# A decoder layer on one Trainium2 core: the expert layer computes for each token its two experts only, in 23 blocks of 128 rows

## The chip, the cores and the metric

The kernel runs on one core of one Trainium2 chip. A core has TensorE (PE, matrix products), VectorE (DVE), ScalarE (ACT), GpSimd (POOL) and SyncE (SP), which issues transfers; POOL issues transfers too. The metric is the device time of one run in microseconds (us), as the median of several runs, lower is better.

## The reference, cut to what matters

One decoder layer over x of 4 batches x 256 tokens x 128 features, all in fp32: self attention with 16 heads and fixed-point rounding, cross attention over a context of 1601 rows per batch with 16 heads of 8 features, and then a gated layer with 8 experts. This change is about the third part, with one edit in the second.

```python
x = x + attention(layernorm(x)); x = x + cross_attention(layernorm(x), ctx)
h = layernorm(x)                                  # 1024 tokens of 128 features
gout = h @ Wgate + bgate                          # 8 numbers per token
topv, topi = top_k(gout, 2); topw = softmax(topv)
combine = sum(one_hot(topi, 8) * topw[..., None]) # two non-zero weights of eight
z = (h @ W1 + b1) * (h @ W2 + b2)                 # per expert, 128 -> 256
g = z @ Wg + bg                                   # per expert, 256 -> 256
o = g * sigmoid(g) * (z @ Wl + bl)
y = o @ W3 + b3                                   # per expert, 256 -> 128
x = x + sum_e combine_e * y_e
```

## The kernel before

The whole layer is one program with a hand-written order on each engine, and semaphores between them. Tokens lie in tiles of 128 on the partitions (8 tiles).

**Self attention** fills the first 260 us or so. At its end ACT looks whether the mask is all zero (`mask_probe`), POOL makes one number of it (`partition_all_reduce`, L573) and then clamps the masks (`mask_clamp`, L579), and PE reads that number into a register (L950) and branches into one of two copies of the cross attention, with and without the mask. The two mask tiles of a batch come by `mask_load` (L566).

**Cross attention** (`cross_attention`) has 16 groups (4 batches x 4 groups of 4 heads). A first pass finds each query row's largest score: PE computes 13 pairs of score chunks per group (`chunks`, L826; 12 full pairs of 2 x 512 keys and a short one of 8 x 65, the thirteenth), and DVE reduces each pair to its maxima (`chunk_maxima`, L1377 and L1379). The pairs go through two PSUM buffers in turn, `pair[0]` and `pair[1]`; a table (`slot_table`) numbers the uses ("slots") on both engines. When a group's 13 pairs are done, DVE takes the row maxima (L1383), POOL splits them into three bf16 parts (`split_maxima`, L588 to L592), four pairs later (`SETTLED`) PE transposes these in a slot of their own (`maxima_T`, L847), DVE copies the result out (`maxima_move`, L1390), and SP writes it under the group's queries (`shift_load`, L488). The second pass, some 22 pairs behind (`LEAD`), recomputes the scores transposed with the maxima subtracted (`tile_scores`, L870), ACT exponentiates them (`tile_exp`, L1167), and PE multiplies with the values (`tile_values`, L895). It is cut into 277 events; three pairs of the first pass are put into every four events. At event `X2_AT` DVE normalises the first three batches for the expert layer. The last batch is finished after the events (`finish_tiles`, L908, L914, L919, with L1404 to L1416 on DVE).

**The expert layer before** is dense: every expert is computed for every token. For each of 8 experts and each of 2 halves of 512 tokens (m = 0..15) PE does `up` (L963, features on the partitions, 512 tokens as columns), ACT adds a bias, DVE multiplies (L1434); `gate_linear` (L972), ACT's SiLU (L1200), DVE (L1440); `down` (L981), and DVE adds the weighted result (`add_expert`, L1448). PE's `up` of the next m is put between the halves of this m's `gate_linear`. The weights of an expert (896 KB) come from HBM by SP into one of two places while the previous ones are used. Gates, top 2 and the combining weights (L996, L1462 to L1487) are computed once at the start of this part, and PE's first products hide them. b3 is added by one extra product with the combining weights (L1012, L1503). Every fp32 product shows as two records in the trace, every transpose as one.

## Time and profile before

| | |
|---|---|
| median of 3 runs | 829.4 us (829.07 to 832.95) |
| profiled execution | 831.66 us, its span 829.6 us |
| PE busy in the span | 684.3 us (82%) |
| DVE busy | 533.8 us (64%) |
| ACT busy | 451.6 us (54%) |
| POOL busy | 133.1 us (16%) |
| mean granted clock of PE | 0.944 of full speed |
| moved by DMA | 52.83 MB |

The span is the time from the first to the last instruction of one profiled execution. Busy shares are means over stages with different limits, so each stage has to be looked at by itself. L12 is line 12 of the kernel before.

### The profile page before, as it was taken

How to read it: one execution, taken by the hardware profiler on the slowest of the kernel's cores; microseconds unless marked ns; L12 is line 12 of the kernel's file. 1: busy time of each engine (PE TensorE's matmuls, PEld its weight loads, DVE VectorE, ACT ScalarE, POOL GpSimd, SP SyncE). 2: the span in 40 equal slices, each digit the busy share in tenths (PEclk: the TensorE clock that was granted, in tenths of full speed). 3: DMA queues.
4: the chain of work that ended last, by engine and by line, in shares of the span. 5: the costliest groups of instructions: out<-in, count | busy, mean ns of one | idle time of the engine just before them, and what ended most of it. 6: DMA issues, size and time to landing. Idle time of an engine off the chain costs nothing.

```text
span 829.6 us, 13514 instructions
## 1 busy us (share of the span) xinstructions
PE 684.3 (82%) x5026; PEld 335.3 (40%) x5026; DVE 533.8 (64%) x868; ACT 451.6 (54%) x766; POOL 133.1 (16%) x167
## 2 busy tenths in 40 slices
PE   2763488888878379998899899899869999999996
PEld 2442255555547033333333333333234554544544
DVE  4377789888896958888888788887033333333332
ACT  2552368888892038876787677778832221122121
POOL 5236601000003522401511140000000000000000
PEclk8796789999999569999999999999889999999999
DMA  6323365445121020106111700001100111101100
GB/s 190 131 68 134 102 224 164 118 118 131 41 76 46 0 79 2 42 2 149 71 42 32 189 2 2 1 2 47 45 2 0 45 45 45 28 16 44 44 1 25
DMA packets 30647, 52.83 MB, mean 64 GB/s; under 512 B 3838, under 2 KB 23882, under 8 KB 30148
## 3 DMA queue, kind: packets, MB, share of 16 engines
q0 software_dynamic: 3424, 26.23, 11.8%
q1 hardware_dynamic: 27172, 25.89, 10.1%
q8 instruction: 35, 0.57, 0.3%
q14 instruction: 16, 0.13, 0.0%
HBM read 39.71 MB, written 12.00 MB: 62 GB/s over the span
## 4 chain that ended last, share of the span: by engine, by line
PE 58%; DVE 25%; ACT 8%; issue 6%; DMA 2%; SPq 0%; DVEq 0%; ACTq 0%
PE pair L972 14%; PE pair L895 11%; DVE smax L1377 10%; PE pair L870 6%; DVE region_p L1286 5%; PE pair L826 5%; PE pair L963 5%; PE pair L981 4%; PE pair L730 3%; DVE region_p L1256 3%; PE pair L694 2%; ACT region_p L1167 2%; ACT region_p L1086 2%; PE pair L716 2%; DVE region_p L1289 1%
## 5 line engine op out<-in xcount | busy, mean ns | idle before, releaser
L1377 DVE TENSOR_REDUCE smax<-pair 128x2 f32<-128x1024 f32 x192 | 225.4, 1220 | 50.1 <-PE pair L826 50.0
L1167 ACT ACTIVATE region_p<-pair 128x1024 f32<-128x1024 f32 (+3 forms) x277 | 217.7, 812 | 63.6 <-PE pair L870 57.9
L972 PE MATMUL pair<-region_p,region_g 128*128 128x512 f32 x256 | 118.7, 607 | 2.5 <-DVE region_p L1440 2.3
L1200 ACT ACTIVATE region_p<-pair,bias_T 128x512 f32<-128x512 f32 x32 | 22.0, 687 | 122.2 <-PE pair L972 122.2
L1440 DVE SCALAR_TENSOR_TENSOR region_p<-pair,bias_T,region_p 128x512 f32<-128x512 f32 x32 | 24.0, 751 | 97.6 <-ACT region_p L1200 97.6
L730 PE MATMUL pair<-ident,region_p 128*128 128x128 f32 x256 | 38.5, 298 | 46.0 <-DVE region_p L1289 46.0
L1256 DVE SCALAR_TENSOR_TENSOR region_p<-region_p 128x1024 int16<-128x1024 int16 (+1 forms) x56 | 67.1, 1220 | 14.0 <-ACT region_p L1072 11.6
L972 PEld LDWEIGHTS pair<-region_p,region_g 128*128 128x128 f32 x256 | 46.6, 192 | 62.5 <-issue 55.1
L895 PE MATMUL pair<-region_p 128*32 128x256 f32 (+1 forms) x832 | 67.6, 398 | 0.5 <-ACT region_p L1174 0.4
L895 PE MATMUL pair<-region_p,v_aug 128*32 128x256 f32 (+1 forms) x832 | 66.5, 391 | 0.4 <-ACT region_p L1174 0.4
L826 PE MATMUL pair<-region_k,qstack 56*128 56x512 bf16 (+1 forms) x256 | 44.2, 365 | 23.9 <-DVE smax L1377 22.5
L963 PE MATMUL pair<-xnT,region_g 128*128 128x512 f32 x128 | 60.9, 598 | 0.0
L1286 DVE TENSOR_SCALAR region_p<-region_p,rnorm 128x256 f32<-128x256 f32 x128 | 59.3, 527 | 1.1
L870 PE MATMUL pair<-qstack,region_k 59*128 59x256 bf16 (+1 forms) x416 | 54.3, 272 | 4.1 <-ACT region_p L1167 2.9
L730 PEld LDWEIGHTS pair<-ident,region_p 128*128 128x128 f32 x256 | 30.3, 151 | 60.3 <-DVE region_p L1289 59.2
L1086 ACT ACTIVATE region_p<-region_p 128x256 f32<-128x256 int16 x128 | 51.3, 409 | 0.0
L1434 DVE SCALAR_TENSOR_TENSOR region_p<-pair,bias_T,region_p 128x512 f32<-128x512 f32 x32 | 24.0, 751 | 32.9 <-ACT region_p L1192 32.9
L1192 ACT ACTIVATE region_p<-pair,bias_T 128x512 f32<-128x512 f32 x32 | 22.0, 687 | 38.3 <-PE pair L963 38.3
L741 PE MATMUL pair<-region_p 128*64 128x256 f32 x256 | 34.7, 392 | 9.8 <-ACT region_p L1094 8.2
L1094 ACT ACTIVATE region_p<-pair 128x1024 f32<-128x1024 f32 x32 | 32.5, 1016 | 15.3 <-PE pair L730 15.3
L716 PE MATMUL pair<-region_p 64*128 64x256 f32 x256 | 38.2, 417 | 2.4 <-ACT region_p L1078 1.8
L1078 ACT ACTIVATE region_p<-pair 128x1024 int16<-128x1024 f32 x32 | 32.7, 1022 | 12.5 <-PE pair L716 12.1
(172 smaller groups left out, 903.3 us busy)
## 6 DMA issues: line engine op xcount, KB each, us to landing
kimg<-region_k SPq DMA_DIRECT2D x56, 200.1 KB
region_k<-kimg POOLq DMA_DIRECT2D x8, 1400.9 KB, 12.4
mask_sb<-in_mask_Bx1xSxS_ff POOLq DMA_DIRECT2D x12, 800.5 KB, 5.2
region_p<-in_mask_Bx1xSxS_ff POOLq DMA_DIRECT2D x4, 800.5 KB, 13.2
region_g<-in_L_ffn_W SPq DMA_DIRECT2D x24, 128.0 KB, 2.2
region_g<-in_L_ffn_Wg SPq DMA_DIRECT2D x8, 256.0 KB, 2.9
region_g<-in_L_ffn_Wl SPq DMA_DIRECT2D x8, 256.0 KB, 3.1
wnat<-in_L_attn_w_qkv SPq DMA_DIRECT2D x8, 192.0 KB, 7.2
```

What stands on the lines that cost most here:

```text
L716: last = pe.matmul(pair[0][:, h * 512 + t * 256:h * 512 + (t + 1) * 256], qf[rows, b * S + t * 128:b * S + (t + 1) * 128], kf[rows, b * S: ...
L730: last = pe.transpose(pair[1][:, c:c + 128], attn[:, b % 2, a:a + 128], ident[:, :])
L826: last = pe.matmul(out_, qstack[b][64 * a:64 * a + KROWS, 2 * g + j, q * 128:(q + 1) * 128], kstack[64 * a:64 * a + KROWS, b % 2, 2 * g + ...
L870: last = pe.matmul(st_bank[n % 3][0:rows, j * 256:(j + 1) * 256], kstack[64 * a:64 * a + SROWS, b % 2, 2 * g + j, keys], qstack[b][64 * a: ...
L895: last = pe.matmul(pair[3][32 * h:32 * h + 32, 512 + s % 2 * S:512 + (s % 2 + 1) * S], v_heads[b % 2][0:rows, t, c:c + 32], pT[0:rows, n / ...
L963: last = pe.matmul(pair[f][:, n * 512:(n + 1) * 512], w[:, u, f * 128:(f + 1) * 128], xnT[:, c * 512:(c + 1) * 512], start=True, stop=True)
L972: last = pe.matmul(pair[2][:, n * 512:(n + 1) * 512], w[:, u, f, half * 128:(half + 1) * 128], zed[:, c, f, :], start=(f == 0), stop=(f == 1))
L1086: last = act.activation(expd[:, b % 2, k * 256:(k + 1) * 256], dotf[:, b % 2, k * 256:(k + 1) * 256], ACT.Exp, scale=1.0 / FXP, accum_out= ...
L1167: act.activation(pT[0:rows, first // 3 % 2, k:k + size], home[0:rows, 0:size], ACT.Exp).then_inc(expt_made, 1)
L1256: return dve.scalar_tensor_tensor(out_, floor16, 0.0, floor16, ALU.is_lt, ALU.add)
L1286: last = dve.tensor_scalar(attn_h[:, b % 2, k * 256:(k + 1) * 256], expd[:, b % 2, k * 256:(k + 1) * 256], rnorm[:, k:k + 1], -0.5, ALU.mu ...
L1377: dve.tensor_reduce(units[:, :, c // 3, c % 3], both, AX.X, ALU.max).then_inc(slot_done, 1)
```

## The change

**Routing.** DVE makes gates, top 2, weights and, new, each token's two row numbers in a buffer in HBM (`route`, in two parts: the first 6 tiles during the last cross attention events, the last 2 after them). The rank of a token inside its expert comes from PE (`ranks`: products of 0/1 matrices in bf16). Expert e owns the rows from 1024 e on. POOL writes each normalised token, with its destination's number behind it as a 129th word, to its two rows by indirect DMA (`dispatch`: 16 transfers of 128 rows; 12 in the first part, 4 in the second). `totals` and some 12 small DVE steps make a table of 23 blocks (the most that 2048 rows in 8 experts padded to 128 can need): first row and expert.

**The blocks.** For each block SP reads its first row into a register and loads 128 rows; PE transposes them, and multiplies them as the stationary side with W1 and W2 side by side (512 columns), with Wg and Wl side by side (2 x 512 columns), and with W3 (2 x 128 columns); the expert's number, read from the table into a register of PE and of DVE, addresses weights and biases. Tokens are now on the partitions, so the biases are added from copies broadcast over all partitions, and z and o are transposed back by PE and moved by ACT. POOL writes each block's 128 result rows to their tokens' places by an indirect DMA. At the end SP reads both results of every token (1 MB), DVE adds them with their weights, and SP writes the output in two halves.

**Weights.** All eight experts are resident: Wg and Wl (4 MB) are loaded by POOL at the start of the cross attention, W1, W2, W3 (3 MB) and the broadcast biases (4 MB) when its fourth batch is under way (`experts_load`, put behind `split_maxima(14)`). To make room, buffers are laid over each other otherwise.

**Filling the buffer.** Before, on POOL: two transfers of zeros over the HBM buffer (4.65 MB together) behind the mask probes of u = 5 and 6, and one transfer of 9088 single words (the numbers of rows that hold no token) behind `mask_load(0)`.

**Short pair fifth.** The short pair of a group (8 x 65 keys) is now the fifth of its 13, and the transposed maxima of the group before are written into the free columns of its buffer: one slot instead of two. The separate maxima slots go; the transpose comes with pair 17 + 13 s instead of behind pair 16 + 13 s.

The core of the diff:

```diff
-SETTLED = 4
+TAIL_AT = 4
+UNITS = tuple(range(TAIL_AT)) + (KT - 1,) + tuple(range(TAIL_AT, KT - 1))
+X2_AT = event_of(2 * (KT * (GROUPS - 2) + KT - 2)) - 2
+XNT_AT, GATE_AT, WEIGHTS_AT, RANK_AT = X2_AT + 5, X2_AT + 9, X2_AT + 12, X2_AT + 14
@@ SP
-            with sp.Fori(1, NE // 2) as r:
-                for u in range(2):
-                    sp.wait_ge(y_mm, 4 * r - 2 + 2 * u)
-                    expert_load(sp, 2 * r + u, u)
+            sp.wait_ge(table_made, 1)
+            sp.wait_ge(dispatched, 16 * 2 * NT)
+            for j in range(NBLK):
+                row = sp.value_load(table[0:1, 0, j:j + 1], min_val=0, max_val=ROWS - 128)
+                if j >= RING_X:
+                    i = j - RING_X
+                    sp.wait_ge(ydisp_written[i % RING_Y], 16 * (i // RING_Y + 1))
+                sp.dma_start(xblk[:, j % RING_X, :], xdisp[bass.ds(row, 128), :]).then_inc(xblk_loaded[j % RING_X], 16)
...
+                    sp.dma_start(ytok[:, k, tiles, :], y_tiles[k, :, tiles, :]).then_inc(ytok_loaded[half], 16)
@@ POOL
+            pool.dma_start(xdisp[:, D:ROW].rearrange("(n p) c -> p (n c)", p=128), pad_index.bitcast(F32),
+                           allow_slow_non_contiguous=True).then_inc(pads_written, 16)
...
+            pool.wait_ge(qstack_made, B)
+            pool.wait_ge(pads_written, 48)
+            for n, w in enumerate((Wg, Wl)):
+                pool.dma_start(wgl.rearrange("p (r f) -> p r f", r=2 * NE)[:, :, n * FF:(n + 1) * FF],
+                               w.rearrange("e (k p) f -> p (e k) f", p=128)).then_inc(experts_loaded, 16)
...
+                for t in range(*FFN_TILES[part]):
+                    for k in range(2):
+                        pool.indirect_dma_start(xdisp, bass.IndirectOffsetOnAxis(ap=slots[:, k, t:t + 1].bitcast(U32), axis=0),
+                                                xrow[:, t, k, :], None, ...).then_inc(dispatched, 16)
+            for j in range(NBLK):
+                pool.wait_ge(yblk_made, j + 1)
+                pool.indirect_dma_start(ydisp, bass.IndirectOffsetOnAxis(ap=xblk[:, j % RING_X, D:ROW].bitcast(U32), axis=0),
+                                        yblk[:, j % RING_Y, :], None, ...).then_inc(ydisp_written[j % RING_Y], 16)
@@ PE
+                    if maxima_with(p) is not None:
+                        last = maxima_T(s - 1, home)
...
+            for j in range(NBLK + 2):
+                if j < NBLK:
+                    up(j)                    # value_load; 1 product of 512 columns
+                if j >= 2:
+                    ogl_transposes(j - 2)    # 2 transposes
+                if j + 1 < NBLK:
+                    block_T(j + 1)           # 1 transpose
+                if 1 <= j <= NBLK:
+                    gate_linear(j - 1)       # 2 products of 512 columns
+                if j < NBLK:
+                    zed_transposes(j)        # 2 transposes
+                if j >= 2:
+                    down(j - 2)              # 2 products of 128 columns
@@ ACT, per iteration
+                ogl_move(j - 2); block_move(j + 1); zed_move(j); gate_silu(j - 1); y_move(j - 2)
@@ DVE
+            def zed_of(j):
+                expert[j] = dve.value_load(table[0:1, 1, j:j + 1], min_val=0, max_val=NE - 1)
+                dve.wait_ge(up_mm, j + 1)
+                chain.step(dve.tensor_tensor(upb, up_bank[j % 2], bias_bc[:, bass.ds(expert[j] * (4 * FF), 2 * FF)], ALU.add))
+                dve.tensor_tensor(zed[:, j % 2, :], upb[:, 0:FF], upb[:, FF:2 * FF], ALU.mult).then_inc(z_made, 1)
+            def gl_bias(j):
+                dve.tensor_tensor(glb[:, j % 2, :], gl_bank[j % 2], bias_bc[...512 columns], ALU.add).then_inc(glb_made, 1)
+            def ogl_of(j):
+                dve.tensor_tensor(ogl[:, j % 2, :], silu[:, j % 2, :], glb[:, j % 2, FF:2 * FF], ALU.mult).then_inc(ogl_made, 1)
+            for j in range(NBLK + 1):
+                zed_of(j); gl_bias(j - 1); ogl_of(j - 1)
```

(In the ACT and DVE loops the bounds on j are left out here.)

## Rows read from the trace of the kernel before

**Rows 1.** Windows: length, busy us of PE, PEld, DVE, ACT, POOL (instructions), clock, DMA.

```profile
304.00:604.00 300.00, 268.49 (x3035) 95.24 (x3033) 226.02 (x253) 225.58 (x297) 52.70 (x99) 0.98 0.17 43
606.50:826.00 219.50, 211.38 (x696) 106.91 (x696) 74.73 (x177) 49.55 (x71) 0.00 (x0) 0.98 0.09 26
```

**Rows 2.** Chain that ended last, stage of the experts: start us, us, what.

```profile
604.11 2.45 issue
...
619.58 5.23 PE pair L972 x8
...
651.41 3.67 PE pair L972 x8
655.08 1.72 PE pair L963 x4
656.80 1.96 PE pair L981 x16
```

**Rows 3.** Groups by line, 304 to 604 us: busy us, mean ns, idle before.

```profile
L847 PE MATMUL pair<-identb,nparts 128*24 128x128 bf16 x15 | 3.3, 217 | 8.7 <-DVE smax L1377 8.7
```

**Rows 4.** Chain in the cross attention.

```profile
395.80 3.72 DMA qstack<-nmT
```

**Rows 5.** Groups by line and form, 606 to 830 us.

```profile
L972 PE MATMUL pair<-region_p,region_g 128*128 128x512 f32 x256 | 118.7, 607 | 2.5 <-DVE region_p L1440 2.3
...
L981 PE MATMUL pair<-region_g,region_p 128*128 128x128 f32 x256 | 32.8, 281 | 0.6 <-DVE region_p L1440 0.4
...
L1448 DVE SCALAR_TENSOR_TENSOR x_in<-pair,comb,x_in 128x128 f32<-128x128 f32 x64 | 18.0, 344 | 7.7 <-PE pair L981 7.7
...
L665 PE MATMUL pair<-ident,xn 128*128 128x128 f32 x2 | 0.4, 302 | 1.3 <-DVE xn L1251 1.3
L1405 DVE TENSOR_TENSOR region_p<-pair,rsum_x 128x256 f32<-128x256 f32 x1 | 0.4, 426 | 0.0
...
L1053 ACT ACTIVATE xnT<-pair 128x256 f32<-128x256 f32 x1 | 0.4, 385 | 0.8 <-PE pair L665 0.8
```

**Rows 6.** Chain: one hand-over from PE by ACT and DVE back.

```profile
680.62 0.70 ACT region_p L1200
...
681.45 0.76 DVE region_p L1440
682.21 0.12 issue
```

**Rows 7.** Groups on DVE, ACT, POOL, whole span.

```profile
L1337 DVE SCALAR_TENSOR_TENSOR region_p<-pair,bproj_fx 128x512 int16<-128x512 f32 x1 | 0.7, 692 | 3.8 <-PE pair L780 3.8
...
L552 POOL DMA_DIRECT2D mask_sb<-in_mask_Bx1xSxS_ff x8 | 4.5, 566 | 122.9 <-ACT mask_sb L1099 95.5 <-DMA kimg<-region_k 27.1 <-POOL v_aug L535 0.3
...
L416 POOL DMA_DIRECT2D v_next<-in_ctx x2 | 2.3, 1138 | 0.6 <-POOL region_p L535 0.3 <-POOL v_aug L535 0.3
...
L573 POOL PARTITION_ALL_REDUCE mask_flag<-mask_any  x1 | 0.4, 378 | 8.2 <-issue 8.2
```

**Rows 8.** DMA issues: KB each, median us to landing.

```profile
region_g<-in_L_ffn_W SPq DMA_DIRECT2D x24, 128.0 KB, 2.2
...
v_next<-in_ctx POOLq DMA_DIRECT2D x2, 768.0 KB, 5.8
...
out<-x_in SPq DMA_DIRECT2D x1, 512.0 KB, 3.2
```

**Rows 9.** Timeline around the flag and PE's register read.

```profile
262.51 8.69 POOL L579 TENSOR_SCALAR mask_sb<-mask_sb 128x1601 f32<-128x1601 f32 x2 [7.18 <-issue]
262.53 3.79 PE L780 MATMUL pair<-wpT,region_g 128*128 128x128 f32 x32
...
266.25 0.60 PE L826 MATMUL pair<-region_k,qstack 56*128 56x512 bf16 x4
```

**Rows 10.** Windows for the clock (columns of rows 1).

```profile
220.00:240.00 20.00, 14.53 (x113) 9.94 (x111) 18.95 (x42) 18.19 (x46) 0.53 (x1) 1.00 0.13 41
...
304.00:310.00 6.00, 6.00 (x20) 1.96 (x18) 1.84 (x2) 0.15 (x1) 0.00 (x0) 0.55 0.00 0
```

More of the change, by code:

```diff
@@ L1033, in _, with block_T @@
-            repeat(pe, NE // 2, two_experts)
+                last = pe.transpose(pair[0][0:NE, t * 128:(t + 1) * 128], comb[:, :, t], ident[:, :])
+            last.then_inc(comb_T, 1)
+            pe.wait_ge(combT_made, 1)
+            for t in range(NT):
+                last = pe.matmul(pair[3][:, t * 128:(t + 1) * 128], combT[:, t, :], b3_sb[:, :], start=True, stop=True)
+            last.then_inc(b3_mm, 1)
+            expert = [None] * NBLK
+            def block_T(j):
+                pe.wait_ge(xblk_loaded[j % RING_X], 16 * (j // RING_X + 1))
+                wait(pe, xblkT_made, j)
+                pe.transpose(xT_bank, xblk[:, j % RING_X, 0:D], ident[:, :]).then_inc(xblk_T, 1)
@@ new lines, in down @@
+            def down(j):
+                pe.wait_ge(oglT_made, j + 1)
+                wait(pe, yblk_made, j)
+                for f in range(2):
+                    last = pe.matmul(y_bank, oglT[:, j % 2, f * 128:(f + 1) * 128],
+                                     w3_sb[:, bass.ds(expert[j] * (2 * D) + f * D, D)],
+                                     start=(f == 0), stop=(f == 1))
+                last.then_inc(y_mm, 1)
+            pe.wait_ge(table_made, 1)
+            pe.wait_ge(experts_loaded, 16 * 9)
```

623 lines of the change are left out of this document (386 added, 237 removed).

## The prediction

> **What bounds the kernel now.** I read the windows first. From 606.5 to 826 us PE is busy 211.4 of 219.5 us [rows 1]: the expert stage is bound by PE, and DVE (74.7) and ACT (49.6) wait for it. The chain of what ended last shows its content: a half of `gate_linear` (8 records) takes 3.4 to 3.7 us, a half of `up` 1.72, `down` 1.96 [rows 2]. Two of each of the first two and one `down` are 12.4 us, and 16 such steps 198 us. The rest is the first 12 us (tail of the last batch, gates) and bubbles. A record of 512 fp32 columns takes 0.43 us (3.44 / 8 or 1.72 / 4), so an fp32 product of 512 columns 0.86; one of 128 columns 2 x 0.12 = 0.245 (1.96 / 8). The cross attention from 304 to 604 us has PE at 268.5 of 300 us, DVE and ACT at 226 each [rows 1]: PE mostly, with stalls of which 8.7 us stand in front of the 15 maxima transposes, each in a slot that waits for DVE [rows 3]. Self attention is hardly touched.
>
> **PE's work in the new expert stage.** Dense means 16 x 512 x 8/8 = 8192 token-expert rows; now there are 23 x 128 = 2944, 36%. Per block: `up` 0.86, `gate_linear` 2 x 0.86 = 1.72, `down` 2 x 0.245 = 0.49, and new five transposes of one record, about 0.11 each, 0.55. Sum 3.62 us, x 23 = 83 us instead of 198.
>
> **But PE will not set the pace; the cycle through the engines will.** A block goes PE, ACT, PE, DVE, PE, ACT, PE, DVE, ACT, DVE, PE, ACT, PE, ACT, POOL. PE's order lets three blocks overlap, but `ogl_transposes(j-1)` stands ahead of `gate_linear(j)` and needs what follows from `gate_linear(j-1)`. That closed cycle is: bias add of 512 columns on DVE 0.69 [rows 7], SiLU of 256 columns on ACT 0.39 (as the copy of 256 columns [rows 5]), product of 256 on DVE 0.43 [rows 5], two transposes 0.24 and `block_T` 0.12 on PE, `gate_linear` until its result is there 3 x 0.43 + 0.61 = 1.90 [rows 5]. Sum 3.77, plus four hand-overs. The chain shows 0.12 to 0.14 between ACT, DVE and PE where registers address operands [rows 6]; I take 0.15 for each, 0.6. Period 4.4 us. DVE's own sum is 2 x 0.69 + 2 x 0.43 = 2.24, ACT's about 1.9, so neither binds. The clock: a stretch with PE busy 14.5 of 20 us had the full 2.4 GHz granted, and a stretch that began cold ran at 0.55 over 6 us [rows 10]. With 3.6 of 4.4 busy I take full clock, after a cold start that costs 3 us.
>
> **One block alone** takes: transpose 0.30, ACT 0.27 (128 columns, an estimate from 0.39 for 256), `up` 0.43 + 0.61, DVE 0.69 + 0.43, two transposes 0.44, ACT 0.39, `gate_linear` 1.90, DVE 0.69, ACT 0.39, DVE 0.43, 0.44, ACT 0.39, `down` 0.65, ACT 0.27 and 13 hand-overs of some 0.08: 9.7 us. Loop: 9.7 + 22 x 4.4 + 3 = 109.5 us.
>
> **From the end of the cross attention to the first block**, in the clock of before. The 2.45 us after 604.11 (PE leaving the branch) stay [rows 2]. The tail of the last batch loses the `up` halves put into it: xn is there at about 614.1 instead of 616.7. Transpose, ACT and the gates of two tiles: 615.5. The routing was hidden behind PE's first products (the 5.23 us piece at 619.58 [rows 2]); now it stands on the path, for 2 tiles instead of 8: some 15 dependent DVE steps of about 0.2 us with ranks between them, 4.1 us: row numbers at 619.6. Four indirect DMAs follow. No row shows one. Nearest below: a plain transfer of 128 rows occupies POOL 0.57 us, one of 1536 pieces 1.14 [rows 7]; above: POOL's only special instruction, 0.38 with 8.2 idle before it, 8.6 [rows 7]. It is nearer to a transfer with 128 pieces whose addresses are read one by one; I take P = 1.2. 12 of the 16 start at about 599.6 (`ranks(0)` stands at event 269 of 277, the events to 604 are 1.06 us each, and DVE has some 9 short steps after it), and are hidden up to P = 20 / 12 = 1.7. So 619.6 + 4.8, landing 2.2 (128 KB [rows 8]): 626.6. Meanwhile DVE makes the table (12 steps of 0.25) and the b3 term (1.2, from 692 ns for 512 columns): hidden, unless P is under 0.6. SP's register read and issue 0.7, landing 2.2: first block at 629.5.
>
> **After the loop:** loop end 739.0; last scatter 1.2 + 2.2; SP issues 4 transfers, 1 MB at the rate of 768 KB in 5.8 us is 7.7 us [rows 8]: 750.1; 8 weighted adds of 0.28 (18.0 / 64 [rows 5]) for the second half 2.3; output 0.4 + 3.2 [rows 8]: 756.
>
> **Cross attention.** Removed: 16 slots. Of the 8.7 us in front of them I count all, since the short pair's slot waits anyway; the DVE copy moves into a slot. Added on PE in the last events: gates 1.5 (12 records of 0.12) and ranks 0.6. The maxima come with pair 17 instead of behind 16: 1.3 us later plus 0.7 for the short pair's reduction. Before, a shift transfer beside a heavy load took 3.72 us and was waited for [rows 4], one of two such waits; now four groups (beside Wg/Wl at 301, keys twice, the 7 MB at 559) may wait 1 us or so more each, half of it caught up. Net -8.7 + 2.1 + 2 = -5 us, between -12 and +4. The 7 MB are issued behind `split_maxima(14)`, 7 POOL transfers of 0.9 to 1.4 us; even at 132 GB/s (768 KB in 5.8 us [rows 8]) they land within 53 us, by 612, ahead of need at 629. What is queued behind them on POOL is `split_maxima(15)`, due a group later (300 / 16, 18 us).
>
> **Filling the buffer.** The two transfers of zeros lie where DMA has room, 18 us each at that rate, and nobody waits. The single words: from 128 to 1536 pieces POOL's time grows by 0.57 us [rows 7], so 9088 pieces cost some 4.2 us of POOL behind `mask_load(0)`. Behind it are the flag and the mask clamps. The clamps start at 262.5 after 7.2 idle, so the flag is made at 255.3, and PE needs it at 266.3 when L780 ends [rows 9]; the clamps count only if a mask is set. So PE loses nothing while POOL loses less than 11 us. The Trainium skill (DMA: Bandwidth & Descriptors, Rules for kernel authors) says that a last dimension that is not contiguous becomes one descriptor per element; by that these are 9088 descriptors, as I count them, and the sum stays. If cover were gone it would cost its 4.2 us; `pads_written` is asked for after the three later query moves, near 300, some 50 us on. Clamps that move beside other DVE steps: +-2. The removed bias transposes at the start: 0.4 us, not counted.
>
> **Sum.** 756 - 5 = 751 in a span of 829.6, thus -78.6. The profiled execution had 831.66 in all, 2.1 over its span, the median is 829.4, 0.2 under it; I apply the difference to the median: 751.
>
> **Register reads.** Each block reads a register from SBUF on SP, PE and DVE. Before has one, on PE: it hid behind L780, whose 3.79 us end at 266.3 as L826 starts [rows 9]. So its price R is between nothing and 3.8 us. On DVE it stands in front of `zed_of`; DVE's round is R + 0.69 + 0.43 + 0.69 + 0.39 + 0.43 + hand-overs 0.3 = R + 2.9, so it binds above R = 1.5. I take under 1.5, since such instructions leave no mark in any row. The Trainium skill (DMA: Bandwidth & Descriptors, Latency and other measured facts) gives a `tensor_load` a floor of about 600 ns; by that page R would be 0.6, DVE's round 3.5 us, and the sum unchanged. No row here shows it.
>
> **Rivals.** (a) Register reads bind: at R = 3.8 the period is 6.7, the loop 22 x 2.3 = 51 us longer: 802; at R = 2.5, 773. For: three engines read in every block. Against: nothing in the trace. 0.13, 772 to 802. (b) The cycle is shorter than I think, because hand-overs are 0.05 as between static instructions, and PE's sum of 3.62 plus 0.2 sets 3.85: 751 - 12 = 739; 0.12, 732 to 740. (c) Indirect DMAs are dearer, P of 2 to 5: dispatch ends at 599.6 + 16 P instead of 624.4, and the last scatter is P - 1.2 longer: P = 2 gives 759, P = 3 776, P = 4.4 800. 0.1 for P over 2. (d) The other side: the same mechanism makes it slower. With P above 4.4 POOL sets both dispatch and loop; start 594.6, 16 P, 5.1 to the first block, 9.7 + 3, 22 P, and P + 15.8 behind: 628 + 39 P reaches 829.6 at P = 5.2; at 8.6 it is about 963. Against it: a plain transfer needs a ninth of 5.2. 0.04. (e) Nothing changes, because PE's savings come back whole as waits: 0.01, the same formula at P = 5.1.
>
> **Chances and range.** Forecast (740 to 770) 0.6, (a) 0.13, (b) 0.12, (c) 0.1, (d) 0.04, (e) 0.01. The range that leaves out no more than 2 in 10 is 735 to 785. The forecast's own is 740 to 770. A measurement of this kernel tells 0.5% from no change. Faster 0.95, same 0.01, slower 0.04.
>
> **What would show it.** Windows over the block loop: PE busy 3.6 us of every 4.4, POOL idle between scatters, clock 1.00 after the first blocks. In the waits: PE on DVE at `ogl_transposes`, not PE on DMA. POOL's indirect DMAs at 1.2 us each; more than 1.7 breaks the dispatch step, a DVE gap in front of L-lines of `zed_of` breaks the register step. In the cross attention: no lone maxima slot, end of the last event 5 us earlier; waits of `tile_scores` on nmT transfers longer would break that step. Wrong by much: the clock at half over the whole loop (PE 7 us per block, 60 us more), or the block loads arriving late because their ring waits for a scatter's landing.

## The result, and the profile after

The changed kernel takes 759.4 us (median of 4 runs, 755.3 to 762.0), beside 829.2 for the kernel before on the same chip. The ratio is 0.9125, with a 95% interval of 0.909 to 0.916: 70 us less. The prediction was 751 us in a range of 735 to 785. The profiled execution is the slowest of the four (762.0 us); it has a span of 760.3 us, 69.3 less than before.

The page's slices of the changed kernel (40 of 19 us; tenths of the clock and of DMA's busy share) show where to look. Slices 31 to 34, which are 570 to 646 us, have PE's clock at 7, 7, 7, 5 tenths, and DMA stands at 5 and 6 in slices 30 and 31.

```profile
PEclk9998779999999966999999999899997775999996
DMA  8333364733577602601180027000056011011103
```

The windows of the changed kernel answer to [rows 1] (same columns): the cross attention, the way to the first block, and the block loop.

```profile
304.00:617.00 313.00, 278.46 (x3047) 99.67 (x3047) 230.59 (x289) 225.75 (x300) 66.64 (x116) 0.95 0.26 74
617.00:642.00 25.00, 11.12 (x61) 8.30 (x61) 10.83 (x50) 6.22 (x9) 11.73 (x13) 0.54 0.12 36
642.00:747.00 105.00, 94.12 (x345) 48.07 (x345) 51.41 (x92) 35.40 (x115) 21.33 (x22) 0.96 0.10 29
```

Behind the cross attention's last group, the expert layer went from 225.9 us (603.7 to 829.6) to 143.3 (617.0 to 760.3). But the cross attention, in which I had forecast 5 us less, is the stage that got longer: ACT copies the sums of its last group out (`group_move`) at 616.98 us, before at 603.72. Against my sum, stage by stage, in us:

| stage | predicted | measured |
|---|---|---|
| end of the cross attention, against 603.7 | -5 | +13.3 |
| from there to the row numbers | 15.9 | 14.9 |
| last dispatch, landed | 7.0 | 7.0 |
| SP's read and load of the first block | 2.9 | 3.0 |
| block loop | 109.5 | 104.5 |
| behind it, to the end of the span | 17.0 | 14.1 |

So the total was right because two errors met: some 18 us lost in the first stage, 9 gained in the others.

The first two rows need a correction. ACT's last exponential ends at 614.28 us and its copy follows only 2.70 us later, released by something that the profile doesn't show; before, the copy follows after 0.76 us. PE's own work isn't later for it: from the last value product to the next transposes it waits 3.4 us whether the copy is late or not. The change and seven of the eleven experiments have this late copy in their traces, the kernel before and the other four don't. So 1.9 us belong to the second row: by its last exponential (602.96 and 614.28) the cross attention ends 11.3 us later than before, and the way to the row numbers takes 16.8. This trace is also a bad one: in two kernels with the change's own code up to there (the lag and the static expert below) that last exponential ends at 610.28, 7.3 us later than before. The stage missed its forecast by 16 us in this trace and by 12 in those.

**The cross attention's loss.** The chain of the changed kernel at group 14 (start us, us, what) shows a shift transfer of 3 KB that takes 7.07 us; one such beside no load takes 1.8. The longest that I had reckoned with was the 3.72 us of [rows 4]. A group has two such transfers; this is its second. In the waits PE stands 6.4 us for it (us in all, times, longest).

```profile
561.86 0.70 DVE smax L1597
...
563.45 7.07 DMA wpT<-nmT
...
570.65 0.61 PE pair L1029 x4
571.26 1.01 PE pair L1054 x8
```

```profile
PE pair L1029 <- DMA wpT<-nmT: 6.6, 2, 6.4
```

The last chain row matters as much: eight records of the value product take 1.01 us here and 0.57 with the full clock. The windows behind the pause have the clock at its lower level (1.2 GHz) with PE busy for 11.05 of 12 us; from 581.7 to 589.5 it was 1.00, and behind a second pause, at 590, the lower level is there again.

```profile
565.70:569.70 4.00, 0.00 (x0) 0.00 (x0) 0.00 (x0) 0.00 (x0) 0.00 (x0) 0.77 1.03 314
569.70:581.70 12.00, 11.05 (x75) 3.18 (x76) 5.94 (x5) 6.06 (x8) 0.00 (x0) 0.51 1.03 343
...
593.70:601.70 8.00, 8.00 (x60) 3.12 (x56) 0.00 (x0) 4.83 (x9) 0.00 (x0) 0.50 0.00 0
```

From group 13's copy to group 16's are 67.3 us (65.4 without the late copy), before 52.7. From the first group's copy to the 13th's are 222.9 us, before 223.2: the edit of the short pair gained next to nothing there in sum.

**The block loop** has the cycle that the prediction describes. One period of the changed kernel's chain:

```profile
693.09 0.70 DVE region_p L1740
...
693.81 0.43 ACT region_p L1419
...
694.26 0.44 DVE region_p L1747
...
694.75 0.44 PE pair L1205 x2
695.18 0.11 PE pair L1172
695.29 1.77 PE pair L1195 x4
...
697.10 0.06 DVEq L1740
```

Bias 0.70, SiLU 0.43, product 0.44, transposes 0.44, `block_T` 0.11, `gate_linear` 1.77 and 0.22 of hand-overs make 4.11 us. The blocks' results leave by 23 indirect DMAs on POOL (the scatters), from 657.66 to 747.00. Their mean distance is 4.06 us, but the last blocks drain faster than the loop runs (3.98, 3.99 and 2.58 us); from the third to the 20th the period is 4.13. The groups by line show the indirect DMAs, which no row of before did: 0.97 us each on POOL, with 0.3 between two that follow each other.

```profile
L794 POOL DMA_INDIRECT ydisp<-region_p x23 | 22.3, 970 | 88.2 <-ACT region_p L1432 88.2
L1734 DVE TENSOR_TENSOR region_p<-pair,region_b 128x512 f32<-128x512 f32 x23 | 15.9, 692 | 16.7 <-PE pair L1179 9.0 <-issue 7.6
```

### The profile page after: what moved, and what is told of

Same layout as the page of the kernel before. It is cut to its first block, busy times and chain, and to the rows that moved or that the text cites. A ratio compares the mean times of both kernels' runs of the same rounds, so it can differ in the third digit from the quotient of the medians.

```text
span 760.3 us, 13411 instructions
## 1 busy us (share of the span) xinstructions
PE 587.9 (77%) x4752; PEld 289.4 (38%) x4752; DVE 534.6 (70%) x885; ACT 443.3 (58%) x818; POOL 191.6 (25%) x234
## 4 chain that ended last, share of the span: by engine, by line
PE 43%; DVE 31%; ACT 9%; issue 8%; DMA 5%; SPq 1%; another core or an unknown queue 0%; DVEq 0%; POOL 0%; ACTq 0%; POOLq 0%
DVE smax L1595 11%; PE pair L1054 10%; PE pair L1029 6%; DVE region_p L1504 6%; PE pair L1195 5%; PE pair L984 4%; PE pair L888 3%; PE pair L852 3%; DVE region_p L1474 2%; ACT region_p L1367 2%; ACT region_p L1286 2%; DVE region_p L1740 2%; PE pair L874 2%; DVE region_p L1507 2%; PE pair L938 1%
## 5 line engine op out<-in xcount | busy, mean ns | idle before, releaser
L1367 ACT ACTIVATE region_p<-pair 128x1024 f32<-128x1024 f32 (+3 forms) x277 | 217.8, 811 | 71.0 <-PE pair L1029 65.4
L1474 DVE SCALAR_TENSOR_TENSOR region_p<-region_p 128x1024 int16<-128x1024 int16 (+1 forms) x56 | 67.2, 1221 | 13.6 <-ACT region_p L1272 11.3
L1054 PE MATMUL pair<-region_p 128*32 128x256 f32 (+1 forms) x832 | 70.6, 414 | 0.7 <-ACT region_p L1374 0.4
L1054 PE MATMUL pair<-region_p,region_b 128*32 128x256 f32 (+1 forms) x832 | 67.8, 398 | 0.2 <-ACT region_p L1374 0.2
L1504 DVE TENSOR_SCALAR region_p<-region_p,rnorm 128x256 f32<-128x256 f32 x128 | 62.1, 549 | 1.1
L984 PE MATMUL pair<-region_k,region_b 56*128 56x512 bf16 (+1 forms) x256 | 44.4, 362 | 23.0 <-DVE smax L1595 21.2
L1029 PE MATMUL pair<-region_b,region_k 59*128 59x256 bf16 (+1 forms) x416 | 54.7, 273 | 8.2 <-ACT region_p L1367 4.0
L888 PEld LDWEIGHTS pair<-ident,region_p 128*128 128x128 f32 x256 | 30.9, 153 | 61.7 <-DVE region_p L1507 60.9
L1195 PE MATMUL pair<-region_g,region_p 128*128 x92 | 44.7, 609 | 0.0
L794 POOL DMA_INDIRECT ydisp<-region_p x23 | 22.3, 970 | 88.2 <-ACT region_p L1432 88.2
L1294 ACT ACTIVATE region_p<-pair 128x1024 f32<-128x1024 f32 x32 | 32.4, 1014 | 16.9 <-PE pair L888 16.9
L1029 PE MATMUL pair<-wpT,region_k 59*128 59x256 bf16 (+1 forms) x208 | 30.3, 302 | 11.3 <-DMA wpT<-nmT 6.6
L1029 PEld LDWEIGHTS pair<-region_b,region_k 59*128 59x128 bf16 (+1 forms) x416 | 22.4, 96 | 37.8 <-issue 15.7
L852 PE MATMUL pair<-xnT,wT 128*128 128x512 f32 x64 | 34.0, 659 | 0.6 <-ACT wT L1266 0.6
L641 POOL DMA_DIRECT2D region_b<-in_mask_Bx1xSxS_ff x8 | 4.7, 583 | 117.2 <-ACT region_b L1299 94.9
```

Of the source, the lines that this page charges most:

```text
L852: last = pe.matmul(qkv_home(hp, c)[:, n * 512:(n + 1) * 512], wT[:, c * 128:(c + 1) * 128], xnT[:, n * 512:(n + 1) * 512], start=True, sto ...
L888: last = pe.transpose(pair[1][:, c:c + 128], attn[:, b % 2, a:a + 128], ident[:, :])
L984: last = pe.matmul(out_, qstack[b][64 * a:64 * a + KROWS, 2 * g + j, q * 128:(q + 1) * 128], kstack[64 * a:64 * a + KROWS, b % 2, 2 * g + ...
L1029: last = pe.matmul(st_bank[n % 3][0:rows, j * 256:(j + 1) * 256], kstack[64 * a:64 * a + SROWS, b % 2, 2 * g + j, keys], qstack[b][64 * a: ...
L1054: last = pe.matmul(pair[3][32 * h:32 * h + 32, 512 + s % 2 * S:512 + (s % 2 + 1) * S], v_heads[b % 2][0:rows, t, c:c + 32], pT[0:rows, n / ...
L1195: last = pe.matmul(gl_bank[j % 2], zedT[:, j % 2, f * 128:(f + 1) * 128], wgl[:, bass.ds(expert[j] * (4 * FF) + f * 2 * FF, 2 * FF)], star ...
```

## The experiments

Eleven kernels ran. Each ratio is to the kernel before on the same chip; the change itself has 0.9125. The same code does not give the same trace time everywhere: the first group's copy lies between 322.4 and 329.2 us in the ten that have the change's code up to there, so stages are compared by differences within a trace. The three copies' distances from group 13 to 16, in us (a star marks the traces with the late last copy, 1.9 us of their last two columns):

| kernel | 13 to 14 | 14 to 15 | 15 to 16 | sum |
|---|---|---|---|---|
| before | 18.3 | 18.1 | 16.3 | 52.7 |
| short pair alone | 18.3 | 18.9 | 16.2 | 53.3 |
| change | 25.5 | 22.2 | 19.6* | 67.3 |
| lag (same code in this stretch) | 24.8 | 19.3 | 19.2* | 63.3 |
| static expert (same code there) | 25.8 | 19.2 | 17.1 | 62.1 |
| single words later (same code there) | 25.6 | 20.5 | 16.9 | 63.0 |
| filled wait | 23.5 | 19.9 | 19.4* | 62.8 |
| one wait | 18.3 | 20.3 | 22.6* | 61.1 |
| weights alone | 25.8 | 21.3 | 19.1* | 66.2 |
| split load | 18.3 | 19.9 | 19.5* | 57.6 |
| split load and lag | 18.3 | 19.4 | 19.1* | 56.7 |
| and Newton | 18.2 | 15.1 | 20.7* | 54.0 |
| and later transposes | 18.3 | 15.1 | 15.5 | 48.9 |

### The load in three parts

```
-                if s == GROUPS - 2:
-                    experts_load()
+                if s >= GROUPS - 3:
+                    pool.wait_ge(shift_loaded, 32 * (s + 1))
+                    weights_load() if s == GROUPS - 3 else biases_load(2 * (s - (GROUPS - 2)))
```

> The changed kernel, but the one load of all experts' weights and biases, which it issues on GpSimd behind the row maxima of group 14, is issued in three parts: the three weight tensors behind the maxima of group 13, two bias tables behind those of group 14, two behind those of group 15, each part only after that group's shift transfer has landed. Theory A (the 7.07 us shift transfer of group 14 is the cause: it was queued with the 7 MB load, TensorE stalled 6.4 us for it and then ran some 30 us at half clock): that transfer takes about 2 us again, the stall is under 1 us, the clock stays full, the cross attention ends at 600 to 603 instead of 617.0, and the kernel takes 745 to 749 us, 10 to 14 less than the change. Rival B (the load slows TensorE and the exchanges whenever it runs, by its traffic into on-chip memory): the loss only moves one group earlier; the time is within 3 us of 759. Rival C (the added gates, ranks and routing of group 14 and 15 cost the 13 us by their own work): no change, 757 to 761.

Ratio 0.903 (0.900 to 0.906), 751.7 us. The transfer of group 14 takes 1.77 us again, and PE waits 1.09 us for it. The chain:

```profile
563.40 1.77 DMA wpT<-nmT
```

By the ratios this is 7.8 us less than the change, by the two traces 9.4. That is under the 10 to 14 of theory A, whose mechanism is shown, but not as the whole loss: the last two groups still take 39.4 us (37.5 without the late copy) instead of 34.5. Nor did PE run some 30 us at half clock, as the expectation has it; in the change's trace it was two stretches of 12 and some 10 us, each behind a pause of its own.

### Three megabytes instead of seven, and one wait

```
                 if s == GROUPS - 2:
-                    experts_load()
+                    weights_load()                       # 3 MB, at the same place
+                if s == GROUPS - 1:
+                    pool.wait_ge(shift_loaded, 32 * (s + 1)); biases_load(0); biases_load(2)
```

> The changed kernel, but where the one load of 7 MB stands, behind the row maxima of group 14 and with no wait, only the three weight tensors (3 MB) are issued; the four bias tables (4 MB) follow behind the maxima of group 15 once that group's shift transfer has landed. Theory A (the shift transfer of group 14 waits for what is queued ahead of it, so its time goes with the bytes): issued 3.8 us behind the first of 3 MB at some 340 GB/s it takes 4 to 5 us, TensorE stalls 3 to 4 us, and half of the loss goes: 754 to 757 us. Rival B (it takes about 7 us whenever any load is on its way, whatever the bytes behind): nothing of the loss of group 14 goes, 757 to 761 us.

Ratio 0.915 (0.910 to 0.920), no better than the change. The transfer takes 7.37 us though less than half of the bytes are there, and lands as the load ends (DMA share 0.50 in the window from 565 us). Rival B holds: the bytes don't set the delay.

```profile
559.97 7.37 DMA wpT<-nmT
```

```
                 if s == GROUPS - 2:
+                    pool.wait_ge(shift_loaded, 32 * (s + 1))
                     experts_load()
```

> The changed kernel with one wait more: GpSimd issues the whole 7 MB load of the experts only once group 14's shift transfer has landed. Theory A (any small transfer that is issued while the 7 MB are on their way is late by some 5 us): the stall of group 14 goes, but the load now lies over group 15's shift transfer, which takes 6 us or more; the stall moves there, and its half clock behind it: 755 to 760 us. Rival B (only a transfer that is issued at the same moment as the load's own issues is late): both groups' transfers take about 2 us, and the time is that of the load in three parts, 749 to 753 us.

Ratio 0.902 (0.895 to 0.908), 750.6 us, like the load in three parts. The transfer of group 15, 12 us into the load, took 6.08 us. But PE waited only 0.96 us for it: it was itself behind by the pause described below. So theory A was right on the transfer and wrong on its price; rival B had the price for a wrong reason.

```profile
572.99 6.08 DMA wpT<-nmT
```

What is common: while the DMA share stands at 1.0, a transfer of 3 KB that otherwise takes 1.8 us takes 6 to 7.4, whether 3 or 7 MB are in all on their way, and whether it is issued with them or 12 us later. Where in the transfer that time lies, its packets tell. SP's transfers go by queue q1 (packets, MB, share); the change from 563.5 to 567.3 us, then from 567.3 to 570.0, and the load in three parts from 563.5 to 565.2:

```profile
q0 software_dynamic: 353, 1.32, 103.1%
```

```profile
q0 software_dynamic: 192, 0.78, 101.2%
q1 hardware_dynamic: 30, 0.01, 1.5%
```

```profile
q1 hardware_dynamic: 30, 0.01, 1.7%
```

So for nearly 4 us behind the issue at 563.45 no packet of it moves, and then all 30 of the group's two transfers go within 2.7 us, beside 192 of the load. In the other two kernels the first packet comes 3.8 us behind the issue. Alone, all 30 are through within 1.8 us of it. If the bytes in front set that first wait, it would differ: but it is the same with 3 and with 7 MB, and with a load that is 5 and one that is 13 us old. What sets it is left open. The Trainium skill (DMA: Bandwidth & Descriptors, Queues, rings and completion order) says that each DMA engine goes round its queues packet by packet. The trace agrees for the second part, where packets of both queues move in the same 2.7 us and the transfer lands 14 us before the load does; for the 3.8 us before it no sentence there prepares.

### PE kept busy during the wait

```
+                        if s == GROUPS - 2 and n % 2 == 0:
+                            for _ in range(54):
+                                pe.matmul(idle, identb, identb broadcast to 256 columns, start=True, stop=True)
                         pe.wait_ge(shift_loaded, 32 * (s + 1))
```

The added matmuls write into a half bank beside running sums, so that one group's sums are changed.

> The changed kernel, but while TensorE waits for the shift transfer of group 14 it does 54 matmuls of 256 columns in bf16 on the identity, whose results nobody reads (about 6 us of work at full clock). Theory A (the stall of 6.4 us on that transfer drops TensorE's clock, and the half clock costs the rest of the 13 us): the transfer still takes about 7 us, but the clock stays at full behind it; of the 13 us that the cross attention ends late, 6 to 8 go: 751 to 753 us. Rival B (TensorE is slow there because the load's traffic holds it up, or the clock falls for another reason): the groups behind the stall stay slow, 758 to 761 us.

Ratio 0.908 (0.904 to 0.912), 753.6 us. The transfer takes 7.14 us as before, PE's wait is filled, and the clock stays at its full level through it and behind it:

```profile
554.80:562.80 8.00, 8.00 (x80) 5.93 (x80) 3.08 (x4) 2.32 (x4) 3.42 (x4) 1.00 1.02 334
562.80:574.80 12.00, 11.06 (x129) 3.83 (x127) 7.17 (x7) 9.54 (x13) 0.97 (x5) 1.00 1.02 342
```

That the pause lowers the clock, and the load's traffic does not, is shown: PE ran at full clock beside the same traffic. The size is not: over the last three groups it took 60.9 us without the late copy, and three kernels with the change's own code there took 61.3, 62.1 and 63.0. How long the clock stays low behind the same pause differs from execution to execution (12 us in the change's trace, about 4 in the lag kernel's), and the change's trace was the worst of them. The interval of the ratio touches that of the change.

### The short pair alone

On the kernel before: `UNITS` and `maxima_with` as in the change, the experts dense, their loads as before.

> The kernel before, with the edit of the short chunk pair alone: it comes fifth in each group and takes the row maxima's transpose into its own slot; the experts stay dense and their weights are loaded as before. Theory A (my prediction's term, 8.7 us of slots saved and 2 us of waits for shift transfers given back): 3 to 7 us faster than the kernel before, 822 to 826. Rival B (as the changed kernel's groups up to 13 show: up to 2.6 us gained, part given back where keys are loaded): 0 to 3 us faster, 826 to 829. Rival C (the shift transfer, which now has fewer pairs to hide behind, is late in every group): slower than before, 830 to 834.

Ratio 0.992 (0.987 to 0.996), 827.4 us. The last copy of the cross attention comes 276.3 us behind the first, before 276.0, and from the first to the 13th it takes 223.0, before 223.2. So in sum the edit gains nothing there, against the 8.7 us that I had counted. The idle time in front of the maxima transposes (7.7 us of it from 327 to 565 us) is gone, but PE now waits for shift transfers. Groups of waits from 304 to 560 us, before in the first fence and with the short pair alone in the second:

```profile
PE pair L870 <- DMA region_p<-nmT: 1.2, 1, 1.2
PE pair L870 <- DMA qstack<-nmT: 0.9, 1, 0.9
```

```profile
PE pair L879 <- DMA region_p<-nmT: 4.6, 4, 2.2
PE pair L879 <- DMA qstack<-nmT: 2.6, 4, 1.1
PE pair L879 <- DMA region_g<-nmT: 0.2, 1, 0.2
```

2.1 us became 7.4, nine waits instead of two. Copy by copy the picture is finer, and the same in all twelve traces that have the edit: ten of the twelve distances up to the 13th copy take 181.0 to 181.5 us together, before 183.5, so 1.9 to 2.4 us are gained. The other two, from the 8th copy to the 10th, take 39.8 us before and anything from 38.5 to 41.9 with the edit, in this kernel 41.9. That is rival B's account (up to 2.6 us gained, part given back). The ratio says some 7 us less all the same, 3 to 11. The first group's copy lies 4.8 us earlier in this trace, but traces of one and the same code lie up to 7 us apart there, so where those 7 us arise is left open.

### The cycle opened

```
-            for j in range(NBLK + 2):        # PE, and the same on ACT
+            for j in range(NBLK + 3):
-                if j >= 2: ogl_transposes(j - 2)      ...      down(j - 2)
+                if j >= 3: ogl_transposes(j - 3)      ...      down(j - 3)
```

> The changed kernel, but a block's own product transposes and down projection come one iteration of the block loop later (three behind its gate and linear products instead of two; one iteration more in all; the ring of transposed rows is 8 instead of 6). Theory A (the period of 4.11 us is set by the closed cycle of gate result, bias, SiLU, product, transposes, next gate result): the cycle is open, the period falls to TensorE's own sum, 3.6 to 3.8 us, and with one iteration more the kernel takes 5 to 8 us less than the change (751 to 754). Rival B (TensorE is already busy 19 of 20 us in the loop, so its own work sets the period): the period stays at 4.0 to 4.1 us and the added iteration costs 1 to 3 us: 760 to 762.

Ratio 0.907 (0.905 to 0.909), 754.7 us: 4.6 us less than the change by the ratios, just short of the 5 to 8 expected. The scatters go from 658.53 to 738.40, 3.63 us apart in the mean, but that isn't the period: with the products behind it one iteration later, the last three blocks leave 2.76, 1.45 and 1.49 us apart. From the third to the 20th the period is 3.91 us, where the change has 4.13. In the chain no other engine is left:

```profile
681.94 1.72 PE pair L1195 x4
683.66 0.22 PE pair L1187 x2
683.88 0.45 PE pair L1213 x4
684.33 1.06 PE pair L1179 x2
685.38 0.22 PE pair L1205 x2
685.60 0.11 PE pair L1172
...
688.10 0.29 issue
```

These six pieces make 3.78 us; in front of every other `up` (L1179) stand 0.14 to 0.29 us in which PE waits for nothing that the profile shows (PE reads the expert's number into its register there; no run tests whether that is the cause). Theory A's mechanism holds, the cycle set the period, though its 3.6 to 3.8 us were not reached and PE looked full before: in 78 us of the loop it was busy 72.7 us in the change (93%) for 19 blocks, and 73.4 here for 21. Matmuls that overlap their neighbours' ends count as busy, so this busy share does not prove a bound; the chain does.

### The expert's number as a constant

`expert[j] = j // 3` on PE and DVE in place of `value_load`: blocks are computed with experts that aren't theirs.

> The changed kernel, but in the block loop TensorE and VectorE take the expert of block j as the constant j divided by 3 instead of reading it into a register from the table; so the blocks are computed with experts that are not theirs, and only the time means something. SyncE still reads the row number of each block. My prediction's step (a register read costs under 1.5 us and is hidden by the wait for the gate products): the period stays at 4.05 to 4.15 us, the time within 1.5 us of the change. My rival a (the register reads are on the cycle): the period falls by the price of a read, 0.4 to 1 us, and the kernel takes 9 to 20 us less.

Ratio 0.909 (0.905 to 0.913), 754.0 us. By the ratios that is 2.8 us less than the change, and the intervals overlap, so the time alone proves little; the period does more: 3.96 us from the third to the 20th scatter instead of 4.13. Neither expectation met it. The read itself is off the cycle, as I had it: the 7.6 us of `issue` in front of L1734 (0.33 for each of 23 blocks, see above) are gone, and only PE is waited for.

```profile
L1734 DVE TENSOR_TENSOR region_p<-pair,region_b 128x512 f32<-128x512 f32 x23 | 15.9, 692 | 7.2 <-PE pair L1179 7.2
```

But the use of the register is on the cycle. In this kernel's chain the piece `DVEq L1740` and the 0.05 behind it are gone, and `gate_linear` is 0.04 shorter:

```profile
694.48 0.02 issue
694.50 0.70 DVE region_p L1740
```

That is 0.12 + 0.04 us per block, all but 0.01 of what the period fell.

### The single words later

```
-            pool.dma_start(xdisp[:, D:ROW]..., pad_index...)      # behind mask_load(0)
             ...
             split_maxima(0)
             pool.wait_ge(x1_made, len(OUT_TILES))
+            pool.dma_start(xdisp[:, D:ROW]..., pad_index...)
```

> The changed kernel, but the transfer that writes the pad rows' 9088 single words is issued on GpSimd behind the first group's split of the maxima instead of right behind the load of the first masks. Theory A (it holds up GpSimd for 3.1 us and the masks' load behind it, so that the clamp of the masks comes 5.2 us later than before and the first pass of the cross attention 1.9 us later): the clamp comes at 262 to 263 us of the trace again instead of 267.7, the first pass 2 us earlier, and the kernel takes 1 to 2.5 us less than the change. Rival B (the clamp's place is set by something else, and the transfer now holds up GpSimd's work for the second batch): no change within 1 us.

Ratio 0.930 (0.926 to 0.933), 771.1 us: 14 us slower than the change. Both theories missed. The clamps do come at 261.99, but they came at 263.96 and 261.59 in two other kernels with the change's own code there, so the place of the transfer explains little of that. What cost time is the mechanism of group 14 once more. The first group's shift transfer now runs beside this transfer of 35.5 KB in 9088 single words and beside two mask transfers of 800 KB each, which POOL issues right behind it (`mask_load(1)`) and which take 17.6 us to land instead of 5.6. It takes 11.72 us, and PE waits 7.24 for it. The chain, and the windows over it:

```profile
300.98 11.72 DMA region_b<-nmT
```

```profile
301.00:306.00 5.00, 3.48 (x16) 1.29 (x16) 3.71 (x4) 1.77 (x3) 0.00 (x0) 1.00 0.72 20
306.00:312.70 6.70, 0.00 (x0) 0.00 (x0) 0.00 (x0) 0.00 (x0) 2.37 (x3) 0.85 0.91 183
```

The first group's copy comes at 334.97 us, in the change at 326.74; that is 8 us of the 14, and where the rest arises is left open. So it isn't the bytes alone that hold up a small transfer: the DMA engines were busy for 0.72 to 0.91 of the time here, but moved 20 and then 183 GB/s, where the experts' load moves some 340. How much of the wait is the words' and how much the masks', which they hold up too, no run separates.

### Both, and then the second pause

> The changed kernel with both edits: the experts' load in three parts behind the shift transfers of groups 13, 14 and 15, and the own product and down projection of a block one iteration later. By the time ratios to the kernel before, the first alone gave 0.903 and the second 0.907 where the change itself gave 0.9125. Theory A (the two causes lie in different stages and add): ratio 0.896 to 0.900, 742 to 746 us by the median of before of 829; 22 block periods of 3.63 us and a cross attention that ends about 10 us before the change's. Rival B (the second's gain was mostly the luck of TensorE's clock behind the stall, which was shorter in its profile than in the change's): no better than the first edit alone, 0.902 to 0.904.

Ratio 0.894 (0.888 to 0.900), 744.7 us; scatters every 3.89 us from the third to the 20th, and 56.7 us for the last three groups. Theory A holds, the two causes add (0.0094 and 0.0056 below the change make 0.8975, inside the interval).

What the last groups still lost has a pause of its own in the middle, there before the change too. ACT needs a square root for the last norm and loads two tables around it. Timeline of ACT and windows, with the load in three parts:

```profile
578.23 1.28 ACT L1253 ACT_TABLE_LOAD   x1
579.90 0.21 ACT L1253 ACTIVATE std<-var_eps 128x6 f32<-128x6 f32 x1 [0.39 <-DVE var_eps L1463]
580.12 1.28 ACT L1370 ACT_TABLE_LOAD   x1
581.42 1.51 ACT L1370 ACTIVATE region_p<-pair 128x1024 f32<-128x1024 f32 x2
```

```profile
579.90:583.90 4.00, 1.40 (x12) 0.39 (x12) 1.87 (x7) 3.73 (x5) 2.64 (x3) 0.77 0.36 98
583.90:587.90 4.00, 4.00 (x30) 1.33 (x27) 0.00 (x0) 1.94 (x4) 0.00 (x0) 0.50 1.03 357
```

```
+                if n == 5:      # 1/sqrt on DVE: a start from the bits, then four times
+                    chain.step(dve.tensor_tensor(t_, y, y, ALU.mult))
+                    chain.step(dve.tensor_tensor(t_, t_, half, ALU.mult))
+                    chain.step(dve.scalar_tensor_tensor(y, t_, 1.5, y, ALU.add, ALU.mult))
-                if e == X2_AT: std_of(5, FFN_TILES[0])      # on ACT
```

> The kernel with both edits, and in addition the standard deviation of the first six tiles of the last norm no longer comes from ScalarE's square root but from twelve small operations on VectorE (a start from the bits and four steps of Newton), so that ScalarE loads no table in the middle of the cross attention. Theory A (the pause of 2.9 us that TensorE makes while ScalarE loads two tables of 1.28 us, and the half clock for 6 to 12 us behind it, are what the last three groups still lose): 4 to 8 us less than with both edits alone. Rival B (VectorE's added operations of some 3 us hold up the chunk maxima, or the clock falls anyway): within 2 us of both edits alone.

Ratio 0.890 (0.885 to 0.895), 739.2 us: 5.5 us less by the medians of one chip, 3.1 by the ratios, where the intervals overlap. The stages are clearer. From group 14 to 15 it takes 15.1 us instead of 19.4, but the next group 1.6 more: PE waits 1.66 us for DVE's later norm, and the clock falls to 0.57 there. The last kernel moves that norm's transposes two events later (`XNT_AT` + 2, gates, weights and ranks + 1) and fills PE before the first block.

> The kernel of the Newton run, and in addition: the transposes of the last norm one step or two later in the cross attention, so that TensorE does not wait for VectorE's twelve operations (1.66 us there, and a half clock for some 4 us behind it), and 20 matmuls of 256 columns in bf16 on the identity behind the product with b3, so that TensorE is busy instead of idle for the 3 to 5 us before the first block arrives. Theory A (a pause in TensorE's work costs itself and a half clock behind it): no pause over 1 us near group 15, TensorE at full clock from the first block on (in the change's trace the first blocks' gate products took 2.2 us and the later ones 1.8), and 3 to 6 us less than the Newton run: ratio to the kernel before 0.883 to 0.886, about 733 to 736 us. Rival B (the clock at the first block is half anyway, or the added matmuls hold up the first transposes): the same time as the Newton run, 738 to 740.

Ratio 0.886 (0.881 to 0.891), 735.7 us (731.8 to 740.7): by the ratios 22 us under the change. The windows over the place of those pauses have the full clock:

```profile
578.00:582.00 4.00, 3.79 (x46) 1.13 (x44) 3.42 (x24) 3.43 (x5) 1.78 (x2) 1.00 0.11 35
582.00:586.00 4.00, 3.62 (x42) 1.57 (x42) 1.63 (x6) 3.29 (x6) 0.83 (x1) 1.00 1.01 351
```

The last three groups take 48.9 us, less than the 52.7 in the kernel before. The other half of the edit did nothing: from the last exponential to the first scatter are 46.4 us, and 46.5 without the added matmuls. They raised the clock for 4 us; then the first two blocks, with PE often waiting, lost it again (0.68 from 629.7 to 633.7 us).

## Why the prediction was right, and where it failed

**PE's work per block, 3.62 us**: 0.16 too low. The chain of the opened loop has 3.78 us of PE per block, with 1.06 for `up` where I had 0.86, and its period is 3.91. That its mean distance between scatters is 3.63 is chance.

**The closed cycle sets the pace**: right, and shown by opening it (4.13 to 3.91). 4.4 predicted, 4.13 measured, 4.06 as the mean that the sum takes 22 times. Hand-overs were over-estimated (0.6 against 0.22), transposes under-estimated (0.24 against 0.44; the same two, L1205, take 0.22 in the opened loop, where PE doesn't stand and wait for them). Rival (b) with its 3.85 was as near, for its reason of short hand-overs, though PE did not set the period.

**P, the indirect DMA**: 1.2 predicted, 0.98 + 0.30 = 1.28 measured. Rivals (c) and (d) are gone. That dispatch took exactly the 7.0 us of the sum is in part luck: 0.8 us pass between the row numbers and the first of the four transfers, which I had not counted, and the last one's own time on POOL lies inside its 2.3 us to landing, where I had added the two.

**Register reads**: hidden, as predicted; rival (a) is gone. I had not priced the registers' use as addresses, 0.16 us in each block, some 3.5 us in the loop.

**Filling the buffer**: 4.2 us of POOL predicted for the single words, 3.1 measured, and nobody waited for them; they took 21.9 us to land.

**Loop fill and clock**: 12.7 us beside the 22 periods predicted, 15.1 measured. The cold start isn't the reason: it cost some 2.7 of the 3 us allowed (the first gate product took 2.04 us where a later one takes 1.77, the first two `up` 2.08 and 2.07 where a later one takes 1.06, and three transposes 0.35 more). But PE's order puts the second block's `up` in front of the first gate product, 1.2 us with its transpose at full clock, which the sum for one block alone left out. The rest isn't traced.

**Behind the loop**: 3 us less. 1 MB landed in 3.7 us and not in 7.7; I had scaled by the slowest row of its kind. Against that, DVE's first add begins only at 753.01, so that all 16 stand behind the landing, 4.5 us and not 2.3.

**The cross attention, -5 us, is the step that failed**, by 16 us in the change's trace and by 12 in two others with the same code there. It had two parts. (1) The 8.7 us of idle time in front of the maxima were counted as gain. The idle time vanished, but only 1.9 to 2.4 us came in, and up to 2.2 went back between the 8th copy and the 10th: the transpose now comes later, the shift transfer with it, and PE waits for that instead (7.4 us in place of 2.1). An idle time that goes is gained only if what is late next is not. (2) "Four groups may wait 1 us or so more each" took [rows 4] with its 3.72 us as the price of a small transfer beside a load. The 7 MB were checked for when they land, not for what else has to move while they do. The transfer took 7.07 us, PE stood 6.4, and the clock fell. By the ratios, putting the load behind the transfer gives back 7.8 us. Of the last two groups' loss (39.9 us without the late copy, before 34.5), 1.7 us (1.44 and 0.24 in the chain) are the gates and ranks of the first six tiles, and the others the longer low clock behind the table pause. The split between these two is argued from rows, not shown by a run. The range of -12 to +4 for this stage excluded what happened. The total came out near because the loop and what is behind it were over-estimated by 8 us; that is luck, not insight.

## What to carry to other kernels

A bulk load is hidden only if no small transfer on a short leash falls into it: list the small transfers that are waited for while it runs, and issue it behind one of them, not in front. An idle time in a profile is worth what the next thing on the same engine allows; follow the moved instruction to its own consumer before counting it. A pause of a few us on PE costs more than itself, so judge it with the granted clock of the windows behind it, and treat a busy share of 93% as no proof that an engine is the bound. The mean distance of a loop's outputs is not its period when the last ones drain faster: take it from the middle of the loop.

## What the runs showed of the hardware that I had not expected

- A 3 KB transfer from SP took 1.8 us alone, 6.1 to 7.4 beside a load at full DMA share whatever its size (3 or 7 MB), of which nearly 4 us passed before its first packet moved, and 11.7 beside 9088 single words and the two mask transfers queued behind them.
- Behind a pause of 3 to 7 us PE was granted the lower of its two levels for 4 to 12 us of unbroken work, and the same code on the same pause got different lengths. A pause filled with unused matmuls kept the full level.
- A vector operation whose operand is addressed by a register starts 0.11 us later (0.06 + 0.05 in the chain); the register read took 0.33 us of DVE (7.6 us for 23 blocks, and none with the constant).
- An indirect DMA of 128 rows holds POOL 0.97 us and 0.30 more before the next; its rows landed in 2.3 us.
- A table load on ACT took 1.28 us. The Trainium skill (ScalarE: Activation LUTs, What ACT_TABLE_LOAD costs) gives the same for the load, and counts some 2.7 us with a drain for every switch to a different set. The trace agrees on the load and shows no such drain: the exponentials start at 581.42 us, right behind the load of 580.12. With PE waiting on ACT the pair of loads stopped PE for 2.87 us and cost the clock behind.
